# One attention loop's context mix in three fp32r passes, with GpSimd splitting and summing, and the last two batches' values as a pair

## The reference, cut to what matters

```python
scores = jnp.einsum('bsghd,btgd->bghst', q, k) * scale
p = jax.nn.softmax(scores, axis=-1)
return jnp.einsum('bghst,btgd->bsghd', p, v)
```

## Time and profile before

| what | value |
|---|---|
| median of 3 runs | 428.82 us (428.65 to 429.05) |
| the profiled execution | 429.2 us |
| its span, first to last instruction | 427.0 us |
| TensorE busy | 417.7 us (98%) |
| VectorE busy | 347.0 us (81%) |
| ScalarE busy | 248.9 us (58%) |
| GpSimd busy | 37.4 us (9%) |

### The profile page before, as it was taken

One profiled execution on the slowest core, in us unless ns is written; L12 is line 12 of the kernel. 1 busy time (PEld: TensorE's weight loads), 2 busy tenths in 40 slices (PEclk: granted clock), 3 DMA queues, 4 the chain that ended last, 5 costly groups with the idle time before them and its releaser, 6 DMA issues.

```text
span 427.0 us, 6939 instructions
## 1 busy us (share of the span) xinstructions
PE 417.7 (98%) x2459; PEld 295.8 (69%) x2465; DVE 347.0 (81%) x705; ACT 248.9 (58%) x780; POOL 37.4 (9%) x58
## 2 busy tenths in 40 slices
PE   7999999999999999999999999999999999999897
PEld 3453455788885767778676686785597799937586
DVE  5789999987999899689899998978986788446831
ACT  2478898788547777748986578564505263220220
POOL 0010000040000001101001000110201015001000
PEclk9999999999999999999999999999999999999999
DMA  7599120500002015993555835698566988530000
GB/s 230 224 188 413 44 93 2 198 2 22 30 2 98 1 51 123 220 295 72 128 124 101 196 70 100 156 205 338 101 121 211 390 297 220 104 123 2 2 2 26
DMA packets 14592, 56.82 MB, mean 133 GB/s; under 512 B 1824, under 2 KB 2912, under 8 KB 13280
## 3 DMA queue, kind: packets, MB, share of 16 engines
q1 hardware_dynamic: 11104, 39.31, 24.9%
q0 software_dynamic: 3456, 17.11, 21.3%
HBM read 41.40 MB, written 0.26 MB: 98 GB/s over the span
## 4 chain that ended last, share of the span: by engine, by line
PE 83%; DVE 9%; ACT 2%; DMA 2%; issue 1%; POOL 1%; SPq 0%; DVEq 0%; ACTq 0%
PE PS L479 11%; PE PS L1840 10%; PE PS L450 9%; PE PS L451 9%; PE PS L452 9%; PE PS L1869 3%; PE PS L1179 3%; PE PS L1313 3%; PE PS L530 3%; PE PS L1855 2%; PE PS L1161 2%; DMA raw_dt.float<-in_wk_nat 2%; PE PS L489 1%; PE PS L1164 1%; PE PS L1165 1%
## 5 line engine op out<-in xcount | busy, mean ns | idle before, releaser
L613 ACT ACTIVATE sq_dt.float<-PS 128x128 bf16<-128x128 f32 x256 | 67.0, 279 | 26.9 <-PE PS L452 20.4
L479 PE MATMUL PS<-s_dt.float,ctx_ring_dt.float 128*128 128x512 f32 x128 | 57.8, 593 | 0.0
L613 ACT ACTIVATION_READ_ACCUMULATOR sq_dt.float<-PS 128x1 f32 x256 | 53.6, 209 | 0.0
L450 PE MATMUL PS<-wkc_dt.float32r,ctx_hi_dt.float32r 128*128 128x512 f32 x128 | 51.5, 403 | 0.1
L451 PE MATMUL PS<-wkT_dt.float32r,ctx_hi_dt.float32r 128*128 128x512 f32 x128 | 50.0, 390 | 0.0
L452 PE MATMUL PS<-wkc_dt.float32r,ctxT_ring_dt.float32r 128*128 128x512 f32 x128 | 50.0, 390 | 0.0
L1840 PE MATMUL PS<-wch_dt.float,xs_dt.float 128*128 128x512 f32 x96 | 42.0, 592 | 0.0
L479 PEld LDWEIGHTS PS<-s_dt.float,ctx_ring_dt.float 128*128 128x128 f32 x128 | 23.6, 190 | 23.6 <-issue 23.0
L695 ACT ACTIVATE luttmp_dt.float<-low_bit_dt.float,vec_dt.float,small_dt.float 128x1536 f32<-128x1536 uint8 x24 | 38.5, 1654 | 2.0 <-DMA lutw_dt.float<-luttmp_dt.float 2.0
L708 POOL DMA_DIRECT2D lutw_dt.float<-luttmp_dt.float x21 | 18.4, 875 | 207.4 <-DVE luttmp_dt.float L702 207.4
L702 DVE SCALAR_TENSOR_TENSOR luttmp_dt.float<-idx_dt.float,luttmp_dt.float 128x1536 f32<-128x1536 uint8 x21 | 36.5, 1755 | 0.0
(11 more groups left out here) (312 smaller groups left out, 859.1 us busy)
## 6 DMA issues: line engine op xcount, KB each, us to landing
lutw_dt.float<-luttmp_dt.float POOLq DMA_DIRECT2D x21, 768.0 KB, 6.2
wch_dt.float<-in_chunks SPq DMA_DIRECT2D x5, 1024.0 KB, 7.9
ctxT_ring_dt.float<-in_ctxT SPq DMA_DIRECT2D x8, 512.0 KB, 3.3
ctx_ring_dt.float<-in_ctx SPq DMA_DIRECT2D x8, 512.0 KB, 3.4
keysT_dt.float<-in_ctxT SPq DMA_DIRECT2D x8, 512.0 KB, 7.2
keys_dt.float<-in_ctx SPq DMA_DIRECT2D x8, 512.0 KB, 8.0
zu_dt.float<-in_wproj SPq DMA_DIRECT2D x1, 2048.0 KB, 7.2
A_first_dt.float<-in_wproj SPq DMA_DIRECT2D x1, 2048.0 KB, 8.0
```

Source lines behind the costliest of these rows:

```text
L450: nc.tensor.matmul(o, x_hi, hi[:, c, :], start=c == 0, stop=False)
L479: last = nc.tensor.matmul(mix_bank(b, c), keysr[k][:, t, c * 128:c * 128 + 128], sS[k][:, t, :], start=t == 0, stop=t == KT - 1)
L613: last = nc.scalar.activation(sq[:, (4 * hf + g) * D:(4 * hf + g + 1) * D], key_bank(b, 2 * t + hf)[:, g * D:(g + 1) * D], ACT.Square, acc ...
```

## The change

Three things change, all in the loop and its end.

1. The mix of batches 1 to 6 becomes three fp32r products per context tile: high context by high weights, high context by low weights, low context by high weights. GpSimd makes the parts for each batch: a cast and a subtraction over the context (1024 elements per partition), and for each of the four weight tiles a cast and a subtraction (512 elements). It also takes over the sum of the four tiles (three additions) from VectorE. The table DMAs of GpSimd are issued between these instructions. Batches 0 and 7 keep the fp32 product; their sums stay on VectorE.
2. To feed this, the exponential of batches 1 to 6 is cut into four tiles and moved ahead of most squares, the first leaf goes ahead of the split of the queries, the sum matmul goes ahead of the second half of the mix, the spread into the middle of it, and VectorE's first table term goes from before the shift to behind the low part of the next context.
3. Batches 6 and 7 get their values as one pair, with the loop's own functions. Two table terms leave the end of the loop: one goes behind the last normalisation, one into the experts, and the last three terms move one expert later.

```diff
@@ loop_pe, step
-                if prev and more:
+                if prev and more and isinstance(b, int) and b == 1:
                     mix(b - 1, 1 - k, 1)
                     total(b - 1)
                     spread(b)
+                elif prev and more:
+                    total(b - 1)
+                    mix(b - 1, 1 - k, 1, range(2))
+                    spread(b)
+                    mix(b - 1, 1 - k, 1, range(2, KT))
@@ mix
+                        if c == 0:
+                            pe.wait_ge(p_split, 4 * b + t - 3)
+                        nc.tensor.matmul(o, keys_hi[:, t, part], p_hi[:, t, :], start=t == 0, stop=False)
+                        nc.tensor.matmul(o, keys_hi[:, t, part], p_lo[k][:, t, :], start=False, stop=False)
+                        last = nc.tensor.matmul(o, keys_lo[k][:, t, part], p_hi[:, t, :], start=False, stop=t == KT - 1)
@@ the end of loop_pe
-            values_of(0, 4, range(G))
-            pe.wait_ge(px_ready, 16)
-            for hf in range(2):
-                values_of(1, 6 if hf else 5, range(4 * hf, 4 * hf + 4))
+            values(3, 0)
+            values(3, 1)
@@ loop_act, step
+                    exponentials(b, k, range(2))
+                    squares(b + 1, 1 - k, 1 if b == 1 else 0)
+                    exponentials(b, k, range(2, KT))
@@ loop_pool
+            def split_keys(b, k):
+                pool.wait_ge(ld_ctx[k], 8 * (b - k) + 16)
+                if b > 1:
+                    pool.wait_ge(pctx, 2 * b)
+                nc.gpsimd.tensor_copy(keys_hi, keysr[k]).then_inc(keys_hi_ready, 1)
+                pool.wait_ge(keys_hi_ready, b)
+                nc.gpsimd.tensor_tensor(keys_lo[k], keysr[k], keys_hi, ALU.subtract).then_inc(keys_split, 1)
...
+            for b in range(1, B - 1):
+                k = b % 2
+                split_keys(b, k)
...
+                high_part(b, k, 0)
+                high_part(b, k, 1)
+                pool.wait_ge(sum_full, b)
+                add_tile(b, k, 1)
+                low_part(b, k, 0)
+                low_part(b, k, 1)
+                for t in range(2, KT):
+                    high_part(b, k, t)
+                    add_tile(b, k, t)
+                    low_part(b, k, t)
+                    if b > 1 and t == 2:
+                        add_terms(pool, b - 1, range(1))
+                if b > 1:
+                    add_terms(pool, b - 1, range(1, 3))
@@ loop_dve, step
-                sums(b - 1, 1 - k)
+                else:
+                    sums(0, 0)
                 maxima(b)
...
-                term(dve, b - 1, 0)
+                    term(dve, 0, 0)
                 shift(b, k)
                 normalise(b - 1, 1 - k)
...
+                if b > 1:
+                    term(dve, b - 1, 0)
                 term(dve, b - 1, 1)
@@ the end of loop_dve
-            term(dve, LUT_STEPS, 1)
-            term(dve, LUT_STEPS, 2)
             dve.wait_ge(r_ready, 8)
...
-            dve.wait_ge(v_full, 7)
-            quantize_heads(6, 4, slice(0, NH))
+            term(dve, LUT_STEPS, 1)
             for hf in range(2):
-                dve.wait_ge(v_full, 8 + hf)
-                quantize_heads(7, 6 if hf else 5, slice(8 * hf, 8 * hf + 8))
+                read_values(3, hf)
+                quantize_values(3, hf)
```

More of the change, by code:

```diff
@@ L335, in build @@
         mx, nm, R = buf("vecs", 512), buf("vecs", 512, skip=512), buf("vecs", 512, skip=1024)
-        ps2 = buf("vecs", 2, 512, skip=1536)
+        ps, ps_pair = buf("vecs", 512, skip=1536), buf("p_hi", 2, 512)
+        p_hi = buf("p_hi", KT, NK, dtype=fp32r)
+        p_lo = [buf("s", KT, NK, skip=k * KT * NK, dtype=fp32r) for k in range(2)]
+        keys_hi = buf("qfront", KT, C, dtype=fp32r)
+        keys_lo = [buf("ctx_ring", KT, C, skip=k * KT * C, dtype=fp32r) for k in range(2)]
         px = buf("px", CT, NH, 64)
@@ L478, in mix @@
                 for t in tiles:
-                    last = nc.tensor.matmul(mix_bank(b, c), keysr[k][:, t, c * 128:c * 128 + 128], sS[k][:, t, :],
-                                            start=t == 0, stop=t == KT - 1)
+                    o, part = mix_bank(b, c), slice(c * 128, c * 128 + 128)
+                    if whole:
+                        last = nc.tensor.matmul(o, keysr[k][:, t, part], sS[k][:, t, :], start=t == 0, stop=t == KT - 1)
+                    else:
+                        if c == 0:
[3 more added lines that the diff above has]
+                        last = nc.tensor.matmul(o, keys_lo[k][:, t, part], p_hi[:, t, :], start=False, stop=t == KT - 1)
                 if t == KT - 1:
@@ L488, in total @@
                 pe.wait_ge(scaled, 4 * KT * 2 - 1 if isinstance(b, int) and b == B - 1 else 4 * b + 7)
-                nc.tensor.matmul(bank(2), ones, ps2[:, 0, :], start=True, stop=True).then_inc(sum_full, 1)
+                nc.tensor.matmul(bank(2), ones, ps, start=True, stop=True).then_inc(sum_full, 1)
             def project_core(parts):
@@ L525, in values @@
                     pe.wait_ge(v_read, 2 * p + 1)
-                else:
+                    if isinstance(p, int) and p == 3:
+                        pe.wait_ge(shifted, 8)
+                elif not (isinstance(p, int) and p == 3):
                     pe.wait_ge(scaled, 28 if isinstance(p, int) and p == 2 else 8 * p + 16)
@@ L564, in loop_pe @@
                 step(2 * i + 1, 1, pair=i - 1)
[L565 to L572, removed]
             step(6, 0, late_pair=2)
@@ L628, in step @@
                     squares(1, 1, 0)
+                if b > 1:
+                    leaf(act, b - 1, 0)
                 if more:
@@ L631, in step @@
                 if b:
-                    for m in range(3):
+                    for m in range(1 if b > 1 else 0, 3):
                         leaf(act, b - 1, m)
@@ L637, in step, with exponentials @@
                     split_context(b + 2, k)
-                if more:
-                    for t in range(1 if b == 0 else 0, KT):
+                if more and b:
+                    if b == 1:
+                        squares(b + 1, 1 - k, 0)
+                    exponentials(b, k, range(2))
+                    squares(b + 1, 1 - k, 1 if b == 1 else 0)
+                    exponentials(b, k, range(2, KT))
+                    for t in range(2 if b == 1 else 1, KT):
                         squares(b + 1, 1 - k, t)
                     key_rstd(b + 1, 1 - k)
-                exponentials(b, k)
+                elif more:
+                    for t in range(1, KT):
+                        squares(b + 1, 1 - k, t)
+                    key_rstd(b + 1, 1 - k)
+                if not (more and b):
+                    act.wait_ge(shifted, b + 1)
+                    nc.scalar.activation(sS[k], sS[k], ACT.Exp, scale=SCALE).then_inc(p_ready, KT)
                 if prev and not more:
                     inverse(b - 1)
-            def exponentials(b, k):
+            def exponentials(b, k, tiles):
                 act.wait_ge(shifted, b + 1)
-                nc.scalar.activation(sS[k], sS[k], ACT.Exp, scale=SCALE).then_inc(p_ready, 1)
+                for t in tiles:
+                    nc.scalar.activation(sS[k][:, t, :], sS[k][:, t, :], ACT.Exp, scale=SCALE).then_inc(p_ready, 1)
             def inverse(b):
@@ L703, in term, with add_terms @@
                                            lutt[:, m, :], ALU.is_equal, ALU.mult).then_inc(lut_term, 1)
-        def add_terms(pool, k):
-            for m in range(3):
+        def add_terms(pool, k, parts=range(3)):
+            for m in parts:
                 pool.wait_ge(lut_term, 3 * k + m + 1)
@@ L911, in loop_dve @@
             score_tiles(7, 1)
-            sums(6, 0)
             maxima(7)
@@ L1463, in tail_pool @@
             deviations_of(8, slice(0, TT))
+            add_terms(pool, LUT_STEPS, range(2, 3))
             pool.wait_ge(ld_w["mask"], 16 * B)
```

87 lines of the change are left out of this document (49 added, 38 removed).

## The result

The changed kernel takes 489.9 us (median of 4 runs, 489.02 to 490.8) against 428.74 (4 runs): a ratio of 1.1427, 95% interval 1.141 to 1.1445. The direction is the forecast's. The size is not: 61 us slower instead of 12, above the range of 419 to 454.

What follows compares the result with a forecast made beforehand. TensorE bounds the kernel, VectorE follows closely. 429.2 - 8.2 (three passes) - 2.1 (loop's end) + 22.2 (VectorE's waits beyond its room) = 441.1, with the median 0.4 below: 440.7 us, slower; 8 in 10 range 419 to 454.

Steps and rivals of the forecast that it cites:

- TensorE's prices: TensorE's mix of a batch: 6.86 us before, 5.44 after as three passes; with the new order, -8.2 us in all.
- the loop's end: After the last mix, with values as a pair: x is updated after 8.4 us instead of 10.54, -2.1.
- "nothing" for the terms moved into the experts: Table terms leaving the loop's end go where VectorE is busy 27.9 of 38 us: no cost, 1.75 us if uncovered.
- the one row L1589: VectorE instruction reading one input from PSUM: ran beside a GpSimd cast in 0.68 us, no longer than L2226's shortest.
- Price of one meeting: Wait when two-input VectorE instructions and GpSimd's go one after the other: 0.48 us, half a mean GpSimd instruction.
- two passes of a cast, one per input (1.04): GpSimd's two-input arithmetic over 512 elements: priced as two casts of 0.52, 1.04 us, giving 12.5 us a batch.
- Its own cap: Upper limit on VectorE's waits for GpSimd: 8.5 us a step, 38.2 us beyond the room in all.
- 1.5 us a step that it must lose: VectorE's idle time in each step: 0.4 us of small gaps and 1.1 for the spread.
- B: Rival: meetings cost little, but a late table term costs 0.4 us in plain steps, up to 3.3; 422 us, chance 0.10.
- A: Rival: meetings are short and fall into VectorE's waits, TensorE stays the bound; 418.6 us, chance 0.25.
- C: Rival: two-input work on GpSimd is as cheap as a cast; no change within about a microsecond, chance 0.13.

Runs made afterwards that it cites:

- the pair alone: The kernel before with only the third part of the change (values of batches 6 and 7 as one pair, later table terms): 426.6 us against 428.6, ratio 0.9955.

## Why the prediction was wrong in size

**Right:** the direction. The bound passed from TensorE to VectorE, as the forecast had it. TensorE's prices were right to a tenth of a microsecond or two in most stretches, 0.4 in the one with weights. So was the loop's end, -1.9 for -2.1, and, within some tenths, "nothing" for the terms moved into the experts: from the update of x to the end the change takes 108.3 us, the kernel before 108.1. VectorE's instructions with an input in PSUM are untouched, as the one row L1589 had said.

**Mis-sized: "Price of one meeting ... I take 0.48".** The run without table DMAs gives it: VectorE busy 176.6 less 127.8 is 48.8 us where the forecast had 34.9; over its 73 counted meetings 0.67 each. One reason is the step before it, "two passes of a cast, one per input (1.04)": 1.27 measured for two inputs of different tiles, and 0.61 for a cast over 512 where 0.52 was taken in proportion. The mean GpSimd instruction is then 1.13, half of it 0.57. The rest is that an instruction behind another waits more than half. The Trainium skill (SBUF — State Buffer, "SBUF: two separate sides") has the later one wait for the whole of the earlier; the three terms of 1.75 each that took 8.38 together agree, and the 32-column instruction of 1.30. The dearest meeting is the product L947, which stands beside GpSimd's longest instruction, the subtraction of 2.35, and took 2.20 in the median instead of 0.69. The forecast counted the roundings as meetings, rightly: in the run without table DMAs they grew by 0.32 to 0.59 on average. Its own cap, 8.5 us a step or 51 in all, came nearer to the 48.8 than the 0.48 that it chose.

**Mis-sized: "1.5 us a step that it must lose".** In the run without table DMAs VectorE is idle 194.7 less 176.6, 3.0 us a step. Here the forecast had taken TensorE at 1.00 throughout. Once TensorE waits for VectorE, its granted clock falls (0.82 to 0.90 in four of these stretches), the same work takes 163.9 instead of 150.0 us, and VectorE, which needs the transposes and the spread, waits in turn. The two terms, 13.9 and 9.1 us, make up the 23.0 by which that run's stretches exceed the forecast's 171.7. That the lower clock causes the longer idle time is argued from the rows, not isolated by a run.

**Failed: "B: meetings cost little, but a table term is late", priced "0.4 us in the plain steps, up to 3.3".** The mechanism was seen, and followed along one way only, from leaf 0 to the maximum. Even there the issue came 18.1 us after the mix in step 3 (163.95 to 182.03) and not "10.9 us", since GpSimd's instructions were longer than priced and were held up by VectorE's. Above all, the other two leaves, whose DMAs are issued at the very end of GpSimd's batch, stand ahead of the inverse and of all the exponentials. The forecast did not follow what is queued behind them, nor that this feeds GpSimd again, and it took 9.1 for the longest landing, where 18.4 came. It also set B beside the meetings as an alternative, while here it comes on top of them: from 465.2 to 490.8, 25.6 us. This is not spread over the steps: 13.6 lie in the stretch from shift 3 to shift 4 (47.9 against 34.3), where the exponentials start 13.5 us late, 10.2 behind the last shift (139.7 us to the end instead of 129.5), where the third leaf's DMA took 18.3, and 2.6 in the other five stretches, less 0.8 by which the first stretch started earlier.

**The rivals.** A needed meetings below 0.30 us each, C two-input work at a cast's price; they cost 0.67 and 1.26 against 0.61.

What stays open: why a table DMA of step 3 took 18.4 us. GpSimd's arithmetic is not needed for it: the kernel before with late DMAs, which has none, shows 15.0 and 18.9 us in the same step. The loads beside it were seen, with the DMA engines' share at 0.99 or more from 184 to 204 us, and so was another table DMA issued 0.6 us ahead; no run took either away.

## What to carry to other kernels

Work handed to an idle GpSimd was paid by VectorE here: price it by VectorE's SBUF-only instructions beside it, each up to a whole GpSimd instruction, and expect the sum to grow faster than GpSimd's time. For the same total, many short GpSimd instructions should cost less than few long ones, by the estimate above; no run isolates that. When an issue moves behind new work in a queue, follow its consumer's queue to the end, with the longest landing beside other loads, and add that cost to the others unless a run shows that they overlap. Ask first what the change is worth if the added work were free: here 4.9 us, of which the pair alone gives 2.0.

## What the runs showed of the hardware that was not expected

- A VectorE instruction of 128x32 took 1.30 us instead of 0.19 beside GpSimd's arithmetic, and one-input bf16 and uint16 roundings grew like two-input ones; over the loop, no VectorE instruction with an input in PSUM grew (0.680 to 0.693 us for the scale of a score tile).
- GpSimd's two-input instruction over 512 elements took 1.04 us in place on one buffer, 1.26 on two tiles; over 1024, 1.89 and 2.35.
- The cost of GpSimd's presence was far from proportional to its time: VectorE lost 12.0 us to 8.8 us of casts a batch, and 27.9 to 12.7 us of mixed work.
- A table DMA that landed in 5.7 to 9.1 us in the kernel before took 18.4 in the change, beside a 2 MB load and another table DMA, and 18.9 at the same place without any arithmetic on GpSimd.
